# Column sums of the first pass: upper and lower squares added on VectorE, three TensorE column sums in place of four

## The reference

```python
h = jnp.concatenate([x[row], bcol[row], edge_attr], axis=1)   # per edge: source row, 0, 64 features
h = jax.nn.relu(_bn(h @ W1 + b1, g1, be1))                    # 256 wide; bn over all edges
ssum = jax.ops.segment_sum(h, col, num_segments=x.shape[0])   # sum by destination
agg = ssum / jnp.maximum(cnt, 1.0)[:, None]
h2 = jnp.concatenate([x, bcol, agg], axis=1)
h2 = jax.nn.relu(_bn(h2 @ W2 + b2, g2, be2))
return jax.nn.relu(h2 @ W3 + b3)
```

## Time and profile before

| | us |
|---|---|
| timed runs, median of 3 | 3201.42 (3198.39 to 3203.39) |
| profiled execution, its own time | 3181.97 |
| its span, first to last instruction | 3180.2 |
| busy in the span: PE, PEld | 2441.9, 914.3 |
| DVE, ACT, POOL | 1393.9, 969.7, 1749.7 |
| mean granted clock of PE | 0.856 |

### The profile page before, as it was taken

The page is one execution under the profiler, slowest core; times in us unless marked ns, Lnnn a source line. Parts: engine busy times, 40 slices in busy tenths (PEclk is TensorE's granted clock), DMA queues, the critical chain, the costliest instruction groups (busy, mean ns, idle before and its releaser), DMA issues. The chain is left out here.

```text
span 3180.2 us, 34295 instructions
## 1 busy us (share of the span) xinstructions
PE 2441.9 (77%) x12138; PEld 914.3 (29%) x12138; DVE 1393.9 (44%) x2299; ACT 969.7 (30%) x1601; POOL 1749.7 (55%) x1850
## 2 busy tenths in 40 slices
PE   4666767657767777777777677777867999999998
PEld 3412112112212222222222122222213433444448
DVE  4422212234323333322333233333223899999878
ACT  3322212112212221222122122212213655655546
POOL 6466666666666666666666666666664222222220
PEclk8888778778878888888888888888876999999999
DMA  8466656666656666666666566566664999999965
GB/s 237 155 210 215 212 194 224 209 221 239 216 194 227 212 213 207 218 204 207 216 229 208 190 223 218 195 228 220 212 206 150 337 350 350 345 343 345 341 238 162
DMA packets 270622, 740.85 MB, mean 233 GB/s; under 512 B 46391, under 2 KB 98661, under 8 KB 270448
## 3 DMA queue, kind: packets, MB, share of 16 engines
q1 hardware_dynamic: 189152, 525.28, 46.2%
q0 software_dynamic: 78432, 212.46, 22.4%
q10 hardware_dynamic: 2864, 0.86, 0.1%
HBM read 501.63 MB, written 236.81 MB: 232 GB/s over the span
## 5 line engine op out<-in xcount | busy, mean ns | idle before, releaser
L621 POOL DMA_INDIRECT sums<-P_d,late x1581 | 1496.5, 947 | 796.4 <-issue 453.3
L1052 DVE TENSOR_TENSOR sums<-psum,sums 128x1024 f32<-128x1024 f32 x396 | 479.0, 1220 | 1524.2 <-remote 823.9
L1351 PE MATMUL psum<-late,sums 128*128 128x512 f32 x1660 | 950.3, 687 | 255.2 <-issue 168.4
L709 ACT ACTIVATE sums<-sums 128x1024 f32<-128x1024 f32 x416 | 437.7, 1054 | 1720.7 <-remote 988.0
L1294 PE MATMUL psum<-sums,ones 128*32 128x512 f32 x830 | 486.5, 667 | 117.8 <-issue 70.2
L1351 PEld LDWEIGHTS psum<-late,sums 128*128 128x128 f32 x1660 | 315.4, 210 | 888.6 <-issue 728.0
L1297 PE MATMUL psum<-sums,ones 128*32 128x512 f32 x830 | 497.9, 676 | 59.5 <-issue 58.6
L1296 PE MATMUL psum<-sums,ones 128*32 128x512 f32 x830 | 494.5, 676 | 36.5 <-issue 35.9
L1295 PE MATMUL psum<-sums,ones 128*32 128x512 f32 x830 | 488.7, 670 | 28.8 <-issue 28.6
L1095 DVE TENSOR_TENSOR late<-late,psum 128x1024 f32<-128x1024 f32 (+1 forms) x407 | 482.6, 1212 | 34.3 <-DMA late<-m_d 32.5
L650 POOL TENSOR_TENSOR late<-dst_f,iota 128x384 f32<-128x384 f32 (+1 forms) x139 | 115.1, 829 | 379.4 <-PE psum L1463 375.3
(11 more groups left out here) (215 smaller groups left out, 2012.0 us busy)
## 6 DMA issues: line engine op xcount, KB each, us to landing
m_d<-sums SPq DMA_DIRECT2D x415, 512.0 KB
late<-m_d SPq DMA_DIRECT2D x406, 512.0 KB, 5.5
sums<-in_ea_main SPq DMA_DIRECT2D x103, 512.0 KB
sums<-P_d,late POOLq DMA_INDIRECT x1581
P_d<-sums SPq DMA_DIRECT2D x24, 512.0 KB
nodes<-in_x SPq DMA_DIRECT2D x24, 256.0 KB
late<-in_x SPq DMA_DIRECT2D x24, 256.0 KB, 3.1
out<-late SPq DMA_DIRECT2D x24, 256.0 KB, 2.4
```

The lines of the kernel that those rows point to most:

```text
L621: pool.indirect_dma_start(out=m_s[s][0:r, k * L:(k + 1) * L], out_offset=None, in_=P1_d, in_offset=bass.IndirectOffsetOnAxis(ap=idx[0:r, G ...
L709: act.activation(q_s[g % Q_SLOTS][0:r, 0:w], m_s[g % M_SLOTS][0:r, 0:w], ACT.Square).then_inc(s_q, 1)
L1052: dve.tensor_tensor(m_s[s][0:r, 0:w], ps_m[place_m[g]][0:r, 0:w], m_s[s][0:r, 0:w], ALU.add).then_inc(s_m, 1)
L1351: ins = pe.matmul(ps_m[place_m[g]][:, 2 * i * L:2 * (i + 1) * L], ea[:, i * P:(i + 1) * P], W1c[:, :], start=True, stop=g not in xg_no, sk ...
```

## The change

- ACT squares the upper half (tiles 2 and 3, columns 512 to 1023) into the PSUM buffer that the add of the group has just emptied, `ps_m[place_m[g]][:, 0:512]`, and the lower half into `q_s`, which is 512 columns wide now. Two activations in place of one.
- DVE has a new step, `half_sums(g)`: q plus the PSUM half, into q; it counts up the new semaphore `s_sums`. It stands in DVE's order behind the add of group g + 1.
- PE's `stats` waits for `s_sums` and has three matmuls in place of four, into three strips. The tail group is as before but for its strip.
- `buffer_free` waits for `s_sums` of the group three entries back, no longer for `s_m`.
- `pick`, `totals` and the waits on `s_pick` follow the three strips.

```diff
-        q_s = [flat[:, 1024 * (M_SLOTS + i):1024 * (M_SLOTS + i + 1)] for i in range(Q_SLOTS)]
+        q_s = [flat[:, 1024 * (M_SLOTS + i):1024 * (M_SLOTS + i) + 2 * L] for i in range(Q_SLOTS)]
...
-        totals = mid[:, 0:L]
+        totals = mid[0:3 * SPAN, 0:L]
...
-            for i in range(4):
-                pool.memset(pick[32 * i:32 * i + 1, i // 2:i // 2 + 1], 1.0 / E).then_inc(s_pick, 1)
+            for i in range(3):
+                pool.memset(pick[SPAN * i:SPAN * i + 1, i // 2:i // 2 + 1], 1.0 / E).then_inc(s_pick, 1)
...
             for g in range(NG):
-                r, w = rows(g), tiles(g) * L
+                r = rows(g)
                 act.wait_ge(s_m, g + 1)
                 if g >= Q_SLOTS:
                     act.wait_ge(s_st, g - Q_SLOTS + 1)
-                act.activation(q_s[g % Q_SLOTS][0:r, 0:w], m_s[g % M_SLOTS][0:r, 0:w], ACT.Square).then_inc(s_q, 1)
+                m, q = m_s[g % M_SLOTS], q_s[g % Q_SLOTS]
+                if g < GF:
+                    act.activation(ps_m[place_m[g]][:, 0:2 * L], m[:, 2 * L:], ACT.Square)
+                    act.activation(q, m[:, 0:2 * L], ACT.Square).then_inc(s_q, 1)
+                else:
+                    act.activation(q[0:r, 0:L], m[0:r, 0:L], ACT.Square).then_inc(s_q, 1)
...
+            def half_sums(g):
+
+                m, q, other = m_s[g % M_SLOTS], q_s[g % Q_SLOTS], ps_m[place_m[g]]
+                dve.wait_ge(s_q, g + 1)
+                dve.tensor_tensor(q, q, other[:, 0:2 * L], ALU.add).then_inc(s_sums, 1)
+
...
                 if g in ranges:
                     ranges[g]()
+                if g >= 1:
+                    half_sums(g - 1)
...
             def stats(g):
 
-                pe.wait_ge(s_q, g + 1)
                 r, m, q = rows(g), m_s[g % M_SLOTS], q_s[g % Q_SLOTS]
-                last = GF - 1
                 if g < GF:
-                    pe.matmul(ps_tot[0:32, :], ones[:, 0:32], m[:, 0:2 * L], start=(g == 0), stop=False, skip_group_check=True)
-                    pe.matmul(ps_tot[32:64, :], ones[:, 0:32], m[:, 2 * L:], start=(g == 0), stop=(g == last), skip_group_check=True)
-                    pe.matmul(ps_tot[64:96, :], ones[:, 0:32], q[:, 0:2 * L], start=(g == 0), stop=False, skip_group_check=True)
-                    ins = pe.matmul(ps_tot[96:128, :], ones[:, 0:32], q[:, 2 * L:], start=(g == 0), stop=(g == last), skip_group_check=True)
+                    first, last = g == 0, g == GF - 1
+                    pe.wait_ge(s_sums, g + 1)
+                    pe.matmul(ps_tot[0:SPAN, :], ones[:, 0:SPAN], m[:, 0:2 * L], start=first, stop=last, skip_group_check=True)
+                    pe.matmul(ps_tot[SPAN:2 * SPAN, :], ones[:, 0:SPAN], m[:, 2 * L:], start=first, stop=last, skip_group_check=True)
+                    ins = pe.matmul(ps_tot[2 * SPAN:3 * SPAN, :], ones[:, 0:SPAN], q, start=first, stop=last, skip_group_check=True)
...
-                    pe.wait_ge(s_xTs if gathered else s_m, i + 1)
+                    pe.wait_ge(s_xTs if gathered else s_sums, i + 1)
```

More of the change, by code:

```diff
@@ L307, in build @@
         t_col = sb("t_col", [P, 2])
-        pick = sb("pick", [P, 2])
+        pick = sb("pick", [3 * SPAN, 2])
         g1_col, be1_col = sb("g1_col", [P, 2]), sb("be1_col", [P, 2])
@@ L367, in build @@
         s_pick, s_half, s_tot, s_fin = sem("s_pick"), sem("s_half"), sem("s_tot"), sem("s_fin")
+        s_sums = sem("s_sums")
         s_eat = sem("s_eat")
@@ L633, in _ @@
             flag = pool.alloc_register("wide_pool")
-            pool.wait_ge(s_pick, 5)
+            pool.wait_ge(s_pick, 4)
             pool.wait_ge(s_m, NG)
@@ L1070, in _ @@
             dve.wait_ge(s_st, NG)
-            dve.tensor_copy(totals, ps_tot[:, 0:L]).then_inc(s_half, 1)
+            dve.tensor_copy(totals, ps_tot[0:3 * SPAN, 0:L]).then_inc(s_half, 1)
             dve.wait_ge(s_half, 1)
-            dve.tensor_tensor(totals, totals, ps_tot[:, L:], ALU.add).then_inc(s_tot, 1)
+            dve.tensor_tensor(totals, totals, ps_tot[0:3 * SPAN, L:], ALU.add).then_inc(s_tot, 1)
             flag = dve.alloc_register("wide_dve")
@@ L1288, in stats @@
             def stats(g):
-                pe.wait_ge(s_q, g + 1)
                 r, m, q = rows(g), m_s[g % M_SLOTS], q_s[g % Q_SLOTS]
-                last = GF - 1
                 if g < GF:
-                    pe.matmul(ps_tot[0:32, :], ones[:, 0:32], m[:, 0:2 * L], start=(g == 0), stop=False, skip_group_check=True)
-                    pe.matmul(ps_tot[32:64, :], ones[:, 0:32], m[:, 2 * L:], start=(g == 0), stop=(g == last), skip_group_check=True)
-                    pe.matmul(ps_tot[64:96, :], ones[:, 0:32], q[:, 0:2 * L], start=(g == 0), stop=False, skip_group_check=True)
-                    ins = pe.matmul(ps_tot[96:128, :], ones[:, 0:32], q[:, 2 * L:], start=(g == 0), stop=(g == last), skip_group_check=True)
-                else:
-                    pe.matmul(ps_tot[0:32, 0:L], ones[0:r, 0:32], m[0:r, 0:L], start=False, stop=True, skip_group_check=True)
-                    ins = pe.matmul(ps_tot[64:96, 0:L], ones[0:r, 0:32], q[0:r, 0:L], start=False, stop=True, skip_group_check=True)
+                    first, last = g == 0, g == GF - 1
[3 more added lines that the diff above has]
+                    ins = pe.matmul(ps_tot[2 * SPAN:3 * SPAN, :], ones[:, 0:SPAN], q, start=first, stop=last, skip_group_check=True)
+                else:
+                    pe.wait_ge(s_q, g + 1)
+                    pe.matmul(ps_tot[0:SPAN, 0:L], ones[0:r, 0:SPAN], m[0:r, 0:L], start=False, stop=True, skip_group_check=True)
+                    ins = pe.matmul(ps_tot[2 * SPAN:3 * SPAN, 0:L], ones[0:r, 0:SPAN], q[0:r, 0:L], start=False, stop=True, skip_group_check=True)
                 ins.then_inc(s_st, 1)
@@ L1372, in _ @@
             pe.wait_ge(s_tot, 1)
-            pe.wait_ge(s_pick, 5)
+            pe.wait_ge(s_pick, 4)
             pe.wait_ge(s_m, NG)
```

## The result

| | before | after |
|---|---|---|
| timed runs, median | 3202.4 us (4 runs, 3198.39 to 3209.08) | 3237.8 us (4 runs, 3228.75 to 3242.64) |
| ratio, 95% interval | | 1.0105 (1.0076 to 1.0134) |
| span of the profiled execution | 3180.2 | 3238.1 |
| last gather starts | 2425.9 | 2479.1 |

The forecast was 3151, the range 3085 to 3275. The time lies in the range, but on the other side: 35 us (24 to 43) lost where 50 were to be won. The slower side had been given 0.32, at 3280. The two profiled executions are further apart, 58 us, since that of before was quicker (3181.97) than any of its timed runs.

A forecast was written before the change was run, and what follows sets the result against it. The first pass was taken as bound by GpSimd's gathers, and by TensorE in slow stretches. Matmul -58, VectorE +5, PSUM buffers +3 and tail +1 gave -49 us: from 3201 to 3151 us, range 3085 to 3275.

The forecast's parts named there:

- The slower side: Whole kernel: slower than before, chance 0.32, mostly from PSUM buffers being freed later; put at 3280 us.
- The floor: First pass: GpSimd needs 1.25 us a gather undisturbed, 1976 us for 1581 gathers.
- GpSimd's 302 us beyond it: First pass: some 302 us lost in GpSimd's waits, all that a change of this pass can win.
- TensorE's slow stretches: First pass: column sums run one behind the other, 3.36 us each, while the other engines stand still until "remote".
- The matmul term: TensorE, first pass: one column sum fewer saves 83 us, of which 0.7 reaches the end, 58 us (33 to 83).
- rival 2: First pass: no change, slow stretches last as long with 12 records a group as with 16; 3201 to 3210, chance 0.11.
- The permission (PSUM buffers): TensorE's edge product: buffer free one period and 0.68 us later, 5.7 us, mostly harmless; cost put at 3 us.
- VectorE's order: VectorE, first pass: half sum behind the add of group g, ahead of counts, ranges and next add; cost put at 5 us.
- Two Squares: ScalarE: one Square of 1056 ns becomes two of 512 columns, 1.19 to 1.60 us, done 0.13 to 0.54 us later.
- The new add: VectorE: 415 half-sum adds of 128x512, one operand in PSUM, 681 ns each, 283 us in all.
- Rival 1: First pass: later-freed PSUM buffers make it slower, each stretch reaching the gathers 2.3 us sooner; +80 us, 3280, chance 0.30.
- the sign that it asked for: TensorE: loads of the edge product wait for the new add in many groups, if the buffers decide.

The follow-up runs named there:

- plain hold: Kernel before, all four column sums kept, with TensorE filling a PSUM buffer only after the next group's add too: 3200.6 us, 1.0030.
- the two SBUF kernels: Changed kernel with squares and half sum in SBUF: buffer free after the group's add, 3188.7 us, 0.9999; only after the half sum, 3230.0 us, 1.0082.
- the swap: Changed kernel with the half sum of group g-1 ahead of the ranges step of group g in VectorE's order: 3218.8 us, 1.0093.

## Why the prediction was wrong

**The floor and where it counts.** The 1.25 us a gather were right to within 0.4%, as the chip of 2844 us shows. GpSimd's 302 us beyond it fit too: there the gathers take 297 us less. That the column sums in TensorE's slow stretches are what makes them was argued from the earlier trace rows and is wrong: three of four removed gave 20 us, and "remote" stayed at 276.

**The matmul term is the step that failed first.** It took "issue" ahead of the column sums' loads as time that would go with the work: 83 us, of which 0.7 reach the end. Its own rival 2 said that a stretch may last as long whatever is in it. Measured for one sum: 5 us (0 to 10); for three: 20. By the rule of the Trainium skill ("TensorE: Matmul & The Clock Gate", Part 3: Packing small matmuls), that such matmuls run at the same time, the removed one is worth nothing; the prediction set against it, and the runs side with the rule to within 5 us.

**The permission (PSUM buffers) was sized at 3 us, and is the dearest term.** The plain hold is 10 (5 to 14), and the wait for the half sum, by the one line between the two SBUF kernels (0.9999 to 1.0082), some 27 us. The argument "TensorE is mostly late by itself, so a later permission is free" is wrong in its second half. A likely reason, not tested: when its signals are late, the products already issued are all that VectorE has once they come, so a group less of lead is a group less to catch up with.

**VectorE's order was misread.** The prediction put the half sum behind the add "and ahead of the counts, the ranges and the next add". The code has it behind `ranges[g]()`. In all groups but a few that is the same; at group 105 it is a wait of 17.9 to 21.6 us for TensorE, 11 to 17 at GpSimd. On the chip without lateness 11.16 us at GpSimd, for 0.30 otherwise, are as much as the whole loss of 10.6. On the others the swap shows no gain (1.0093 for 1.0105), and waits of 12 to 15 us stand there without the change too.

**What was right.** Two Squares: 601 + 613 = 1.21 us, between the bounds 1.19 and 1.60, at the lower end. The Trainium skill's estimate ("ScalarE: Activation LUTs", What ACT_TABLE_LOAD costs), 1.22 us for both, agrees. But two in a row overlap in the trace (starts at 1490.37 and 1490.90), so a pair is done after 1.14 us, 0.08 later than the one Square of 1.06 before and less than the 0.13 that the prediction had as its least. The new add is 679 ns for a forecast 681. Rival 1 named the mechanism and that the kernel gets slower, and the sign that it asked for is there: the edge product's load waits for the new add, 497 us in all (a weak sign, as the plain hold has 538 at 10 us). Its price of 80 us was more than twice the measured 35. It had each slow stretch reach GpSimd 2.3 us sooner, and GpSimd's waits until "remote" did not grow (85 for 88, 248 us for 255).

**The sum as measured**, on the chips of 3200 us, from one kernel to the next: column sum -5; half sum and later column sums +4 (0.9985 to 0.9999); TensorE's wait for the half sum +27 (0.9999 to 1.0082); the Squares and the add in PSUM +7 (1.0082 to 1.0105), inside the intervals. That makes 33 of 35 (24 to 43), where the prediction had -58 + 5 + 3 + 1. Of the 27 the plain hold explains 10. What makes the rest of it stays open: the half sum's release is an add of 0.68 us later than that of the next group's add and stands behind the ranges step. The first was not varied alone, and half sums ahead of the ranges step gained nothing that could be measured. What makes the signals late on some chips stays open as well.

## What to carry to other kernels

Idle time that a trace calls "issue" is not a saving until a run shows that someone waits for it: take one instruction out and time that before a design is built on it. When a result moves to a buffer that another engine wants back, find each long step of the queue in which the releasing instruction now stands, and count the lead in groups at that one place; an average period hides it. Whether the release stands ahead of the next group's main step or behind it counts for more than how late it is: 1.1 us later but ahead of the next add cost nothing (1.0004), behind the add 0.3%, behind the add and the half sum 0.8%. And before one long wait in a trace is put down to a change, look for it in the traces of kernels that lost nothing.

## What the runs showed of the hardware

- The same kernel took 3187 to 3207 us on four of the chips whose number was known and 2844 us on two. Of the difference 297 us are the first pass, 2280 us of gathers against 1983, with 255 us of "remote" idle time at GpSimd against none, and 35 us the stage ahead of it (145.9 against 110.9). Behind the last gather both take 753 to 754 us.
- On the slower chips steps that wait for TensorE start up to 18 us after the records of their matmuls end (1472.2 to 1490.4 in the lines above), and then several engines start together. VectorE had gaps of 1.2 to 1.3 us between the small operations of its ranges step there. One to four column sums a group, two to six slots for the squares, seven or eight for the gathers: GpSimd had 60 to 108 waits until "remote" with indirect gathers, 88 in the earlier trace rows.
- With plain loads in place of the gathers such a chip ran the pass in 1301 us and the kernel in 2207, and in that execution the lateness was left only ahead of the pass, where the gathers are indirect. The changed kernel with plain loads took 1343 and 2215 us on a chip without lateness.
